# BitNet tiles: the result product of five tiles placed behind the next tile's gate product, its addition behind VectorE's product

## What is computed

```python
def bitlinear(x, w):
    return jnp.einsum('bsh,oh->bso', act_quant(x), weight_quant(w))

def h_bitlinear(x, w):
    return jnp.einsum('bsh,oh->bso', act_quant(fwht(x)), weight_quant(w))
gate = bitlinear(x, w_gate)
up = bitlinear(x, w_up)
intermediate = jax.nn.silu(gate) * up
return h_bitlinear(intermediate, w_down)
...
x = x + jnp.tanh(g_xattn[0]) * _L0_xattn_ref(_layernorm(x), ...)
x = x + jnp.tanh(g_ffn[0]) * _L0_ffn_ref(_layernorm(x), ...)
x = x + jnp.tanh(g_xattn[1]) * _L1_xattn_ref(_layernorm(x), ctx_2048, ...)
x = x + jnp.tanh(g_ffn[1]) * _L1_ffn_ref(_layernorm(x), ...)
```

## Time and profile before

| | |
|---|---|
| median of 3 runs | 576.94 us (575.88 to 577.8) |
| the profiled execution, its own time | 575.66 us |
| its span, first to last instruction | 573.8 us |
| busy: TensorE, VectorE, ScalarE, GpSimd | 94%, 67%, 61%, 55% |
| mean granted clock of TensorE | 0.987 of full speed |
| DMA, mean over the span | 171 GB/s |

### The profile page before, as it was taken

One profiled execution on the slowest core, in us unless ns is written; L12 is line 12 of the kernel. 1 busy time (PEld: TensorE's weight loads), 2 busy tenths in 40 slices (PEclk: granted clock), 3 DMA queues, 4 the chain that ended last, 5 costly groups with the idle time before them and its releaser, 6 DMA issues.

```text
span 573.8 us, 9599 instructions
## 1 busy us (share of the span) xinstructions
PE 540.4 (94%) x3232; PEld 465.2 (81%) x3232; DVE 387.3 (67%) x822; ACT 349.2 (61%) x719; POOL 313.7 (55%) x311
## 2 busy tenths in 40 slices
PE   2999988998989999999999999999999899799997
PEld 2787757777778898999999999999899788577886
DVE  6858985689856676555555667556664765677882
ACT  3642243756587868666566756656766664677882
POOL 1697337799177788542345433335787545762320
PEclk9999998999999999999999999999999998799999
DMA  8611234410157666777977586734445654345651
GB/s 279 242 56 55 108 125 135 148 37 1 57 201 237 213 223 196 233 223 261 276 236 238 190 283 207 247 118 148 156 175 146 215 170 136 87 142 184 217 183 38
DMA packets 67248, 97.88 MB, mean 171 GB/s; under 512 B 6400, under 2 KB 38912, under 8 KB 67200
## 3 DMA queue, kind: packets, MB, share of 16 engines
q1 hardware_dynamic: 67200, 97.26, 52.2%
HBM read 68.28 MB, written 28.97 MB: 169 GB/s over the span
## 4 chain that ended last, share of the span: by engine, by line
PE 76%; DVE 7%; ACT 6%; POOL 6%; issue 3%; DMA 1%; DVEq 0%; ACTq 0%; POOLq 0%
PE ps L1523 22%; PE ps L1524 21%; PE ps L1525 21%; PE ps L1624 4%; PE ps L1729 2%; PE ps L1713 2%; PE ps L1736 1%; ACT q2T L902 1%; PE ps L1742 1%; POOL ex_lo L572 1%; DVE e_r L1449 1%; DVE xr L1180 1%; DMA xr<-in_x 1%; ACT probs L939 1%; ACT kv_w_hi L810 1%
## 5 line engine op out<-in xcount | busy, mean ns | idle before, releaser
L645 POOL TENSOR_TENSOR probs<-probs,rsum 128x512 f32<-128x512 f32 x64 | 66.4, 1041 | 79.0 <-DVE rsum L1232 78.9
L1227 DVE TENSOR_REDUCE nmax<-ps 128x2 f32<-128x512 f32 x64 | 44.1, 689 | 39.7 <-PE ps L1525 39.4
L1025 ACT ACTIVATE e_hi<-e_r 128x512 fp32r<-128x512 f32 x64 | 40.3, 630 | 34.3 <-DVE e_r L1449 33.5
L939 ACT ACTIVATE probs<-ps,nmax 128x256 f32<-128x256 f32 x128 | 59.7, 479 | 0.2
L572 POOL TENSOR_TENSOR kv_w_lo<-blk_raw,kv_w_hi 128x1024 fp32r<-128x1024 f32 x17 | 41.2, 2424 | 27.3 <-ACT kv_w_hi L810 27.3
L1449 DVE SCALAR_TENSOR_TENSOR e_r<-ps,cw_row 128x512 f32<-128x512 f32 x64 | 43.6, 685 | 16.4 <-PE ps L1525 14.4
L1223 DVE TENSOR_TENSOR oT_lo<-ps,oT_hi 128x512 fp32r<-128x512 f32 x32 | 22.1, 692 | 41.9 <-ACT oT_hi L949 41.9
L1218 DVE TENSOR_TENSOR pT_lo<-ps,pT_hi 128x512 fp32r<-128x512 f32 x64 | 43.8, 685 | 8.9 <-ACT pT_hi L945 8.3
L945 ACT ACTIVATE pT_hi<-ps 128x512 fp32r<-128x512 f32 x64 | 38.3, 600 | 18.6 <-PE ps L1624 18.5
L764 POOL TENSOR_TENSOR e_lo<-e_sq,e_hi 128x512 fp32r<-128x512 f32 x19 | 24.6, 1292 | 42.8 <-ACT e_sq L1031 37.9
L949 ACT ACTIVATE oT_hi<-ps 128x512 fp32r<-128x512 f32 x32 | 19.1, 597 | 42.6 <-PE ps L1525 42.6
(11 more groups left out here) (291 smaller groups left out, 1851.6 us busy)
## 6 DMA issues: line engine op xcount, KB each, us to landing
cw_row<-cw_scratch SPq DMA_DIRECT2D x64, 256.0 KB, 3.5
v_hl<-v_scratch SPq DMA_DIRECT2D x24, 512.0 KB, 3.7
blk_raw<-in_w_blocks SPq DMA_DIRECT2D x23, 512.0 KB, 3.8
k_hl<-k_scratch SPq DMA_DIRECT2D x18, 512.0 KB, 4.1
k_scratch<-kv_out SPq DMA_DIRECT2D x32, 256.0 KB, 2.7
v_scratch<-kv_out SPq DMA_DIRECT2D x32, 256.0 KB, 3.2
v_scratch<-kv_hi SPq DMA_DIRECT2D x24, 256.0 KB, 2.3
blk_raw<-in_w_tail SPq DMA_DIRECT2D x10, 512.0 KB, 4.7
```

Of the source, the lines that this page charges most:

```text
L645: nc.gpsimd.tensor_tensor(probs[:, b, :, :], probs[:, b, :, :], rsum[:, b, :].unsqueeze(2).to_broadcast([P, 2, S]), ALU.mult).then_inc(pro ...
L939: last = nc.scalar.activation(probs[:, b, t, :], ps[:, S_BANK[b], t * S:(t + 1) * S], ACT.Exp, bias=nmax[:, b, t:t + 1], accum_out=esum[:, ...
L1025: nc.scalar.activation(e_hi[i % 4][:, :], e_r[i % 2][:, :], ACT.Square).then_inc(e_hi_done, 1)
L1227: V.tensor_reduce(nmax[:, b, :], ps[:, S_BANK[b], :].rearrange("p (t k) -> p t k", t=2), AX.X, ALU.max, negate=True).then_inc(max_done, 1)
```

## The change

In TensorE's order D moves, in steps 4 to 8, from the end of the step (tile i-3) to behind G (tile i-4). Tiles 0 to 4 are done this way; from step 8 on the old place holds again for tiles 5 to 7. In VectorE's program the addition of these five tiles moves likewise from behind `fT_lo` to right behind the product of the step (in step 8, which has no product, ahead of the largest value of tile 6). `bn_stats` follows at the end of that step, in step 8 for two tiles, and one wait for VectorE's own last instruction is added in step 7.

```diff
-        STAGES = [("G", 0), ("U", 0), ("H", 2), ("C", 3), ("F", 1), ("D", 3)]
+        STAGES = [("G", 0), ("D", 4), ("U", 0), ("H", 2), ("C", 3), ("F", 1), ("D", 3)]
         FFN = [("Q", 0)]
         for i in range(NT + 2):
             if i == GN - 1:
                 FFN.append(("Q", 1))
             for u, behind in STAGES:
-                if 0 <= i - behind < NT:
+                if 0 <= i - behind < NT and (u != "D" or behind == 4 and i <= NT or behind == 3 and i >= NT):
                     FFN.append((u, i - behind))
...
+            def add_tile(n):
+                dve.wait_ge(y1_filled, n + 1)
+                dve.wait_ge(dve_step, steps[0])
+                V.scalar_tensor_tensor(xr[:, n, :], ps[:, pair_of["C", n], 0:D], am2[:, n % 2, 3:4], xr[:, n, :],
+                                       ALU.mult, ALU.add).then_inc(y1_taken, 1)
+
...
                 if i == 0:
                     quantise(1)
+                if 4 <= i <= NT:
+                    add_tile(i - 4)
                 if 0 <= i - 2 < NT:
...
-                if 0 <= i - 3 < NT:
-                    n = i - 3
-                    dve.wait_ge(y1_filled, n + 1)
-                    dve.wait_ge(dve_step, steps[0])
-                    V.scalar_tensor_tensor(xr[:, n, :], ps[:, pair_of["C", n], 0:D], am2[:, n % 2, 3:4], xr[:, n, :],
-                                           ALU.mult, ALU.add).then_inc(y1_taken, 1)
+                if i >= NT:
+                    add_tile(i - 3)
...
-                if 0 <= i - 3 < NT:
-                    dve.wait_ge(y1_taken, i - 2)
-                    last = stats(i - 3)
+                for n in [i - 4] * (4 <= i <= NT) + [i - 3] * (i >= NT):
+                    dve.wait_ge(y1_taken, n + 1)
+                    last = stats(n)
                 if i == NT - 1:
+                    own(last)
                     factors_begin(0, GN)
```

## The result

The changed kernel takes 590.35 us (median of 6 runs, 587.08 to 594.27); the kernel before, run beside it, 576.41 us (573.88 to 577.8). A second set of four runs gave 592.17 us and 1.0275 (1.0234 to 1.0316). The sign was forecast, the size was not: 585.0 and a range up to 590.0 stood against it. The runs of the changed kernel also lie 7 us apart, those of the kernel before 4 us.

A forecast was written before the change was run, and what follows sets the result against it. TensorE carries 76% of the chain of waits. +9.14 us in steps 4 to 7 less 1.0 on VectorE gives +8.1: execution 575.66 to 583.8, and 585.0 for the median, which lies 1.3 higher; range 582 to 590.

The forecast's parts named there:

- the ring: Steps 4 to 7: H waits for silu, product and addition, a stall once in every period; 9.14 us in all.
- The 8.84 of step 5: Later period: H's load to q2T 3.01, to silu's end 4.14, then product, addition, H; 8.84 us against 6.78, +2.06.
- no credit for D behind G: TensorE, tiles 0 to 3: D's 0.24 us wait goes, U still waits for q; credit 0 to 0.24 per tile, 0 taken.
- step 8: VectorE, steps 7 and 8: line 1074 shorter once GpSimd's split has ended; bounds 0 and -1.4 us, -1.0 taken.
- The sum, +9.14 - 1.0: Whole kernel: steps 4 to 7 less VectorE's gain in steps 7 and 8, +8.1 us, execution 583.8, median 585.0.
- q2T spaced 8.8 to 9.2 us: Sign in the new profile: ScalarE's q2T copies 8.8 to 9.2 us apart instead of 6.78.
- granted clock 1.00 in the stretch: Sign in the new profile: TensorE's clock stays full, granted clock 1.00, in the stretch the change touches.
- the rival: TensorE's clock falls in each of the four stretches, 1.7 us of full-rate work lost each, +6.9, 591.9 us; 12%.
- the hidden wait: H's wait for `y1_taken` is hidden behind U and D's 0.24 us are gained: 575.0 us, faster; 3%.
- the planner's pairs: Planner hands out the same pairs, H2 to H5 following C0 to C3; rival, H draws another: 576.9 us, 2%.
- nothing was given back: Rival: attention's start is set by something that does not shift, half given back, +4, 581; 3%.

The follow-up runs named there:

- the filled kernel: Changed kernel with six matmuls of 512 columns, results unread, put in TensorE's gap ahead of H in steps 4 to 7: 585.65 us, ratio 1.0173.
- The product alone: Kernel before with only TensorE's order changed, D behind the next tile's G, additions left behind fT_lo: 576.47 us, ratio 1.0007.
- the two filled kernels: Changed kernel with six or with two matmuls in each gap ahead of H: 585.65 us (1.0173) and 584.45 us (1.0155).
- the wait alone: Kernel before, orders untouched, plus one wait: H of tiles 2 to 5 goes only when VectorE's product of tile n+2 is done; 586.02 us, ratio 1.0187.
- the first profile: Profiled execution of the changed kernel, nothing altered: 589.82 us, periods of steps 4 to 7 10.72, 10.44, 10.72, 10.51 us.
- the second: Profile of the changed kernel timed once more, nothing altered: median 592.17 us, ratio 1.0275, periods 10.71, 8.88, 9.18, 11.70 us.
- one tile: Kernel before with the change for tile 0 only (its D and its addition moved), tiles 1 to 7 as before: 580.07 us, ratio 1.0069.
- The half-microsecond filler: Changed kernel with two matmuls (0.43 us together) instead of six in each gap ahead of H: 584.45 us, ratio 1.0155.

## Why the prediction was wrong

**Right: the ring.** H waits for `y1_taken` behind silu, product and addition. The forecast periods were 6.78 + 2.32, 8.84 and twice 9.16 us, 36.26 in all; the filled kernel, whose clock stayed at 1.00, has 9.14, 8.82, 9.17 and 9.23, 36.36. The sum of +9.14 us was off by 0.1. key_high and value_high, waited for by nobody before, were to add 0.32 us each; measured are 0.35 and 0.41 (9.17 and 9.23 against 8.82).

The 8.84 of step 5 came out right partly by luck. The prediction let silu end 4.14 us after q2T and took VectorE's row to be no later, though its own sums say 4.21 against 4.18. In the new order G is done earlier and silu follows `q` directly: it ends 3.95 us after q2T. VectorE's row (fT_lo, clip, `bn_stats`) lets the product go at 4.15, and so the period stayed where it was forecast. In steps 6 and 7, with a copy ahead of silu, silu is the later one again.

**Right: no credit for D behind G.** The product alone is worth nothing (1.0007), since U waits for q.

**Right in mechanism, off in what is left: step 8.** VectorE's chain got 1.00 us shorter by line 1074 and its neighbours, as taken; 0.3 of it was given back by tile 7's q2T. Without the clock the change then isn't +8.1 but +8.5 us by these rows (9.24 less 0.70), and the two filled kernels, +8.9 and +10.0 by their ratios (lower ends +6.6 and +8.6), lie there or a little above.

**Wrong: the weight of the clock.** The sum, +9.14 - 1.0, has no term for the clock, and two signs of the prediction's list did not come, "q2T spaced 8.8 to 9.2 us" and "granted clock 1.00 in the stretch". The step that failed is the reason given for leaving it out, the rival's sentence "Against it: around the new gap stand full-rate products on both sides", and the 12% drawn from it. All three profiles with the additions behind the product of tiles 4 to 7 and the gap left empty have two to four falls, and so has the kernel with the wait alone; the full-rate products around the gap did not keep the clock up. The price in the rival, 1.7 us for each fall and 591.9 us for four, was near (1.28 to 1.62 measured in the first profile, 1.57 and 2.47 in the second; 590.35 and 592.17 us), and the clock's part of the first profile, 6.03 us, is the term that the sum lacked. The range stopped at three falls.

What the trace of the kernel before would have allowed, with two gaps that the prediction did not look at, and under them the second of these gaps in the changed kernel:

```profile
168.96 0.63 PE L1624 MATMUL ps<-eye,probs 128*128 128x128 f32 x4 [1.55 <-DVE kv_out L1258]
...
492.15 0.80 PE L1523 MATMUL ps<-hT_hi,kv_w_lo 128*128 128x512 f32 x1 [3.21 <-DVE s_sq L1277]
```

```profile
505.88 0.51 PE L1528 MATMUL ps<-hT_hi,kv_w_lo 128*128 128x512 f32 x1 [3.22 <-DVE s_sq L1277]
```

Behind the 1.55 us the clock stayed at 1.00 (windows from 168 to 172 us), in the 3.21 us it fell (0.78 from 490 to 492 us, 0.50 in the two behind), and around the two gaps of 1.26 and 1.20 us it fell as well. The new gap, 1.8 to 2.1 us in one piece, lay between what kept its clock and what lost it, and ought to have been given about even odds, with a range up to 592. Even that would not have been a rule by length: the same 3.2 us gap kept its clock in the changed kernel's first profile (1.00 from 504 to 514 us).

That these falls are caused by the gaps is shown by filling them: eight periods in two kernels, no fall. Which gap ends in a fall is not settled. Counted over the profiles here: the gap of 1.7 to 2.1 us ahead of H ended in one in 12 of 17 cases (4 of 4, 2 of 4, 3 of 4, 2 of 4 with the wait alone, 1 of 1 with one tile), the one of about 1.5 us at attention's start in none of 11, the one of 3.2 to 3.5 us late in the run in 9 of 11. "TensorE: Matmul & The Clock Gate" in the Trainium skill, section "What's actually happening", has the clock follow recent activity; the filled gaps agree with it. The half-microsecond filler agrees too, but I had expected it to be too little.

The other rivals: the hidden wait did not come, the planner's pairs were as listed, and nothing was given back behind step 8 beyond single tenths.

## What to carry to other kernels

A wait for a buffer has a price by what stands ahead of its releaser in that engine's queue: moving a 0.5 us addition behind a product of the same step put silu, product and addition between two TensorE stages, 2.3 us in each period. Look for the rotation that hands a stage's buffer to the next user before moving the instruction that frees it, and for the slack that it has today. And when TensorE gets a new gap of some 2 us, price the clock's fall with it; a few matmuls into a bank that is free anyway can be cheaper than the gap left empty.

## What was not expected of the hardware

Two matmuls of 512 columns (0.43 us) in a gap of about 2 us were as good as six against the fall of the clock, in all four gaps. And the fall is a matter of the run, not of the schedule: with gaps equal to 0.02 us, one profile had four and the other two, one of them longer, and the two profiles differ in later falls too (0.83 between 390 and 400 us in the second alone). A gap as long as 3.2 us kept its clock in two of the eleven profiles. Differences of 1.6 us between two executions of this kernel can be one such fall.
